# Routed experts' weights in two transfers per expert (8 KB and 4 KB a partition) in place of three of 4 KB

## The reference, cut to what matters

```python
E, K, H, I, CAP = 32, 6, 512, 256, 192
...
xb = jnp.zeros((E, CAP + 1, Hd), x.dtype).at[eid, pos].set(h_rep)
g = jnp.einsum('ech,eih->eci', xb, w_gate)
u = jnp.einsum('ech,eih->eci', xb, w_up)
inter = jax.nn.silu(g) * u
yb = jnp.einsum('eci,ehi->ech', inter, w_down)
y = yb[eid, pos] * w_slot[:, None]
routed = y.reshape(-1, K, Hd).sum(axis=1)
...
x = x + 0.5 * ffn(layernorm(x)); x = x + attention(layernorm(x)); x = x + 0.5 * ffn(layernorm(x))
```

## Time and profile before

| | us |
|---|---|
| median of 3 runs | 1623.55 (1618.26 to 1630.44) |
| the profiled execution's own time | 1628.87 |
| its span, first to last instruction | 1626.6 |
| TensorE busy | 1474.5 (91% of the span) |
| VectorE busy | 1106.5 (68%) |
| ScalarE busy | 1026.9 (63%) |
| GpSimd busy | 777.3 (48%) |
| weight transfers, issue to landing, median of 192 | 6.2 |

### The profile page before, as it was taken

One profiled execution on the slowest core, in us unless ns is written; L12 is line 12 of the kernel. 1 busy time (PEld: TensorE's weight loads), 2 busy tenths in 40 slices (PEclk: granted clock), 3 DMA queues, 4 the chain that ended last, 5 costly groups with the idle time before them and its releaser, 6 DMA issues.

```text
span 1626.6 us, 23865 instructions
## 1 busy us (share of the span) xinstructions
PE 1474.5 (91%) x8434; PEld 1235.5 (76%) x8436; DVE 1106.5 (68%) x2094; ACT 1026.9 (63%) x2046; POOL 777.3 (48%) x655
## 2 busy tenths in 40 slices
PE   5999989999993889999999999986999989999995
PEld 4877778888882678887887888775787769888884
DVE  5659868776682466766666677664658878886873
ACT  6861548877682467666667666663864338887873
POOL 0113245656764666656556656520113234657564
PEclk9999999999997799999999999999999999999998
DMA  7736479999985101111111121103764549999994
GB/s 278 242 121 206 115 269 325 263 275 254 262 219 88 53 27 40 40 51 54 39 41 52 46 91 46 39 27 110 256 203 146 150 158 306 300 292 257 292 235 62
DMA packets 113204, 257.59 MB, mean 158 GB/s; under 512 B 21216, under 2 KB 22176, under 8 KB 112832
## 3 DMA queue, kind: packets, MB, share of 16 engines
q1 hardware_dynamic: 90560, 204.16, 38.1%
q0 software_dynamic: 22528, 51.92, 15.4%
HBM read 187.27 MB, written 68.76 MB: 157 GB/s over the span
## 4 chain that ended last, share of the span: by engine, by line
PE 38%; DMA 12%; POOL 5%; DVE 5%; issue 3%; ACT 3%; DVEq 1%; POOLq 0%; ACTq 0%; SPq 0%
DMA out<-e_y,slots 11%; PE a_bank L90 4%; PE a_bank L92 4%; PE a_bank L91 4%; POOL out L931 4%; PE a_bank L1615 3%; PE a_wide L1606 2%; PE a_wide L1603 2%; PE a_wide L1607 2%; PE a_bank_o L90 2%; PE a_bank_o L92 2%; PE a_bank_o L91 2%; DVEq L1430 1%; PE d_ps_gate L90 1%; PE a_bank L1582 1%
## 5 line engine op out<-in xcount | busy, mean ns | idle before, releaser
L1022 DVE TENSOR_TENSOR e_w_lo<-e_raw,e_w_hi 128x1024 fp32r<-128x1024 f32 x192 | 234.3, 1221 | 30.2 <-ACT e_w_hi L957 30.2
L1539 POOL TENSOR_SCALAR t_prob<-t_prob,t_inv 128x128 f32<-128x128 f32 (+7 forms) x128 | 111.7, 872 | 222.9 <-DVE t_inv L1437 222.7
L957 ACT ACTIVATE e_w_hi<-e_raw 128x1024 fp32r<-128x1024 f32 x192 | 202.3, 1055 | 0.0
L924 POOL DMA_INDIRECT e_xg<-htab,slots x128 | 148.7, 1162 | 73.6 <-issue 35.1
L1096 PE MATMUL e_ps_gate<-e_xt,e_w_hi 128*128 128x384 f32 x512 | 165.9, 387 | 0.0
L406 POOL TENSOR_SCALAR d_inter<-d_inter 128x512 f32<-128x512 f32 x32 | 26.4, 825 | 262.6 <-DVE d_inter L537 262.4
L931 POOL DMA_INDIRECT x_after_ffn<-e_y,slots x64 | 107.7, 1682 | 91.4 <-DMA x_after_ffn<-e_y,slots 80.5
L1096 PE MATMUL e_ps_up<-e_xt,e_w_hi 128*128 128x384 f32 x512 | 151.2, 360 | 0.0
L931 POOL DMA_INDIRECT out<-e_y,slots x64 | 103.7, 1621 | 85.5 <-DMA out<-e_y,slots 74.8
L1327 ACT ACTIVATE t_prob<-a_wide,t_neg_max,a_q_scale 128x128 f32<-128x128 f32 (+7 forms) x128 | 106.5, 832 | 55.6 <-DVE t_neg_max L1431 55.4
L1097 PE MATMUL e_ps_gate<-e_xt,e_w_lo 128*128 128x192 f32 x512 | 133.1, 260 | 0.0
(11 more groups left out here) (218 smaller groups left out, 4464.0 us busy)
## 6 DMA issues: line engine op xcount, KB each, us to landing
e_raw<-in_w_experts SPq DMA_DIRECT2D x192, 512.0 KB, 6.2
htab<-d_h SPq DMA_DIRECT2D x16, 1024.0 KB, 5.2
d_x<-in_x SPq DMA_DIRECT2D x16, 512.0 KB, 6.9
d_xs<-in_x SPq DMA_DIRECT2D x32, 256.0 KB, 3.6
x_after_ffn<-d_xs SPq DMA_DIRECT2D x32, 256.0 KB, 3.3
q_x<-x_after_ffn SPq DMA_DIRECT2D x32, 256.0 KB, 3.0
t_res<-x_after_ffn SPq DMA_DIRECT2D x32, 256.0 KB, 2.7
x_after_attention<-t_res SPq DMA_DIRECT2D x32, 256.0 KB, 2.0
```

Source lines behind the costliest of these rows:

```text
L924: pool.indirect_dma_start(xg[e % GATHERED][q][:, :], None, htab, row).then_inc(gathered[e % GATHERED], 16)
L957: act.activation(third(w_hi[e % 2], c), third(raw[e % 3], c), ACT.Copy).then_inc(hi_ready, 1)
L1022: dve.tensor_tensor(third(w_lo[e % 2], c), third(raw[e % 3], c), third(w_hi[e % 2], c).bitcast(F32), ALU.subtract).then_inc(lo_ready, 1)
L1539: pool.tensor_scalar(prob[:, u, 0:width(i)], prob[:, u, 0:width(i)], inv[:, u:u + 1], 1.0, ALU.mult, ALU.mult).then_inc(p_ready, 1)
```

## The change

The thirds are no longer one transfer each. `LOADS` has two pieces: columns 0 to 2047 (gate and up, 8 KB a partition, 1 MB) and 2048 to 3071 (down, 4 KB a partition, 512 KB). SP issues two transfers an expert. The first one of expert e+3 waits until thirds 0 and 1 of expert e are split (`lo_ready` at 3e+2), the second until third 2 is (3e+3). The splits stay three; those of thirds 0 and 1 both wait for the first transfer. There are 2 semaphores in place of 3 for each buffer.

```diff
--- before.py
+++ after.py
@@ -65,6 +65,7 @@
 NO_SLOT = 4000.0
 SBUF_END = 229344
 THIRD = WALL // 3
+LOADS = (slice(0, WGU), slice(WGU, WALL))
 WORK_AT = SBUF_END - 2 * 4 * WALL - 4 * 8 * NT * E
 GATHERED = 5
 WQKV = KB * 6 * DH
@@ -383,8 +384,7 @@
             spot()
             for u in range(2):
                 sp.wait_ge(up_ready, FB * (PLACES - 2 + u) + FB)
-                for c in range(3):
-                    part = slice(c * THIRD, (c + 1) * THIRD)
+                for c, part in enumerate(LOADS):
                     sp.dma_start(raw[u][:, part], a["w_experts"][u, :, part]).then_inc(w_loaded[u][c], 16)
                 spot()
             sp.wait_ge(w_done, 1)
@@ -896,21 +896,21 @@
         @block.sync
         def _(sp):
             def load_weights(e, c):
-                sp.dma_start(third(raw[e % 3], c), third(a["w_experts"][e, :, :], c)).then_inc(w_loaded[e % 3][c], 16)
+                sp.dma_start(raw[e % 3][:, LOADS[c]], a["w_experts"][e, :, LOADS[c]]).then_inc(w_loaded[e % 3][c], 16)
 
             def load_chunk(c):
                 sp.dma_start(xs[c % XS][:, :], attention_chunks[c][2]).then_inc(att_loaded[c % XS], 16)
 
             sp.wait_ge(done.dense, FB * G)
             sp.wait_ge(gathered[1], 32)
-            for c in range(3):
+            for c in range(2):
                 load_weights(2, c)
             for c in range(min(XS, len(attention_chunks))):
                 sp.wait_ge(y_stored[c], 16 * ((NT - 1 - c) // XS + 1))
                 load_chunk(c)
             for e in range(E - 3):
-                for c in range(3):
-                    sp.wait_ge(lo_ready, 3 * e + c + 1)
+                for c in range(2):
+                    sp.wait_ge(lo_ready, 3 * e + c + 2)
                     load_weights(e + 3, c)
                 if XS <= e + XS - 2 < len(attention_chunks):
                     sp.wait_ge(att_split, e - 1)
@@ -953,7 +953,7 @@
         @block.scalar
         def _(act):
             def split(e, c):
-                act.wait_ge(w_loaded[e % 3][c], 16 * (e // 3) + 16)
+                act.wait_ge(w_loaded[e % 3][c // 2], 16 * (e // 3) + 16)
                 act.activation(third(w_hi[e % 2], c), third(raw[e % 3], c), ACT.Copy).then_inc(hi_ready, 1)
 
             def turn(e):
@@ -1677,7 +1677,7 @@
                 staged = [staged_buffers(nc, places, "place", PLACES - 2 + u, n) for u in range(2)]
                 raw = [nc.alloc_sbuf_tensor_at(f"e_raw{u}_{n}", [P, WALL], F32, offset=staged[u][0]) for u in range(2)]
                 xs = [places.enter_context(nc.sbuf_tensor(f"d_xs{u}_{n}", [P, D], F32)) for u in range(XS)]
-                w_loaded = [[own_semaphore(nc, k, f"e_w_loaded{r}{c}_{n}") for c in range(3)] for r in range(3)]
+                w_loaded = [[own_semaphore(nc, k, f"e_w_loaded{r}{c}_{n}") for c in range(2)] for r in range(3)]
                 y_stored = [own_semaphore(nc, k, f"d_y_stored{u}_{n}") for u in range(XS)]
                 done = front(nc, block, a, k, n, normed, acc, (x1, out), htab, slots, staged, raw, xs, w_loaded, y_stored)
                 routed_experts(nc, block, a, k, n, htab, acc, slots, raw, xs, w_loaded, y_stored, done)
```

## The result

The changed kernel takes 1649.06 us (median of 4 runs, 1640.26 to 1657.33) against 1622.68 for the kernel before (4 runs). The ratio is 1.0144, 95% interval 1.0107 to 1.0181: slower, by some 23 us by the ratio and 26.4 us by the medians. The profiled execution has a span of 1644.7 us against 1626.6, so it shows 18.1 us of the loss.

The account below looks back on a forecast made before the run. The prediction took the ring of scatter landings to bound the expert loops. It summed (0.36 - 0.08) x 49 loops = +13.7 us on the median of 1623.55, giving 1637 us, with a range from 1603 to 1664.

Parts of the forecast that it names:

- What bounds the kernel: Expert loops: a ring of waiting for landings and issuing two scatters, 9.01 us each in FFN 0, 8.72 in FFN 1.
- Items 1 to 3: SP's weight loads and ScalarE's splits: fewer issues, a later first half, and splits awaiting 1 MB; each worth 0.
- leaves later: First half of gate and up is issued 1.60 us later; worth 0, tightest margin 2.1 us in FFN 0.
- Item 4: Weight transfers: larger packets have less overhead, -0.08 us a loop, 3.9 us at most over 49 loops.
- Item 5: Scatters beside weights: longer packets hold them up; +0.36 us a loop taken, between 0 and 0.66, upper end 0.88.
- A: Expert loops: scatters held up a little more, +13.7 us, 1637 us; own range 1626 to 1656; chance 0.40.
- The mechanism inside item 5: Shared engines: a scatter is held up by some 8.5 weight packets, half of an expert's packets becoming 155 ns longer.
- The sign that would have put the gathers into the ring: TensorE waiting much more for gathers while scatters land no later would refute placing gathers outside the ring.
- B: Expert loops: only the packet-overhead saving counts, scatters do not notice packet size; -3.9 us, 1620 us; chance 0.22.
- C: Expert loops: the second scatter finds a gap in the respaced loads; -21 us, 1602 us; chance 0.21.
- D: Queue q0, both expert loops: the scatter loses every engine turn, landings above 6.9 us; +39 us, 1663 us; chance 0.14.
- E: Splits wait for late weights as the 2.1 us margin fails; some 5 to 10 us, once; chance 0.03.

Follow-up runs that it names:

- the repeat: The changed kernel itself, run once more beside the kernel before; 1650.10 us, ratio 1.0194.
- three_2k: Kernel before with the weights laid out in HBM as six blocks of 2 KB rows, same three transfers; 1621.03 us, ratio 0.9993.
- one_4k_later: Changed kernel with one 1.5 MB transfer an expert in 4 KB packets, issued when third 1 of the next expert is split; 1633.68 us, ratio 1.0039.
- late3: Kernel before, but the transfer of third 0 waits until third 1 is split, as in the changed kernel; 1629.60 us, ratio 1.0039.
- even_odd_8k: Kernel before with gate and up loaded as even and odd partitions in 8 KB rows, both when third 1 is split; 1624.07 us, ratio 0.9986.
- two_4k: Changed kernel with weights in 4 KB blocks in HBM, so the 1 MB transfer has 4 KB packets; 1631.65 us, ratio 1.0068.
- one_12k: Changed kernel with one 1.5 MB transfer an expert in 12 KB rows, issued when third 2 is split; 1630.45 us, ratio 1.0040.
- one_2k: Changed kernel with one 1.5 MB transfer an expert in 2 KB packets (six blocks in HBM); 1647.00 us, ratio 1.0127.
- one_4k: Changed kernel with one 1.5 MB transfer an expert in 4 KB packets, issued when third 2 is split; 1614.88 us, ratio 0.9941.
- halves_8k: Kernel before with gate and up loaded as partitions 0 to 63 and 64 to 127 in 8 KB rows, when third 1 is split; 1734.83 us, ratio 1.0683.

## Why the prediction was right, and where it was not

*What bounds the kernel*: right. The changed kernel's loss has the size of the growth of the wait for landings, in both profiled executions (19.0 us of waits for 18.1 of span, 14.0 for 13.6 in the repeat), the halves' loss is mostly there too, and without weights the loops fall to TensorE's 7.99. In small steps the two do not always go together: `three_2k` waits 16.5 us less than the kernel before with a span 6.4 shorter, `one_4k_later` waits the same with a span 4.5 longer.

*Items 1 to 3, worth nothing*: right for waits on loads (0.0 us before line 957, the 2.1 us of margin held). But "leaves later" was priced as lateness alone. `late3` shows 5 to 6 us from the new moment by itself, barely clear of nothing, and `even_odd_8k` with the same timing shows none. That is the likely missing part of the sum: a load that nobody waits for can still collide.

*Item 4, -0.08 a loop*: nothing in the runs shows it as a gain; it is below what they can tell.

*Item 5, the term that carried the forecast*: the sign was right and `two_4k` shows that the long packets of this transfer are its larger part. The size was off. It was put at +0.36 a loop, with item 4 at 0.28 or 13.7 us. Measured were 18.7 us in the 49 loops of one execution, 0.45 a loop in FFN 0 and 0.31 in FFN 1, and in the repeat 0.12 and 0.51, so the share of either FFN is not to be trusted. The loss is some 23 to 26 us by the first measurement, 24 to 31 by the repeat: 12 to 20 of it go with the packets, 7 to 11 with the moment and the one large transfer. 12 to 20 us over 49 loops are 0.25 to 0.41, so the packets' term was about met. That is luck: 0.36 was chosen between 0 and 0.66, and the count of packets behind it is not what the runs show. One slip in the recorded sums: the upper end of A's range, +32, is 0.66 x 49 without the 0.08 of item 4; with it the end is +28. The first measurement lies under both.

*The mechanism inside item 5* was too simple. It had each scatter held up by so many packets of such a length. The median landing stayed at 6.3 us in one execution (6.4 to 6.8 were expected) and was 6.6 in the repeat. What grew in both is the mean landing of the second scatter, with more long ones among them, and about a third of that is a single engine that finishes late while others idle. `even_odd_8k` shows that length alone is not enough, `one_12k` that the loss does not grow with the length as was expected (15.6 us for 35 to 60), and `one_2k` that shorter is not always better. What about the 1 MB transfer of 128 rows of 8 KB makes scatters land late is open; so is whether it is the order in which an engine gets the rows, or the partitions that they go to.

*The other signs*: the loops of FFN 1 took 9.03 us (8.9 to 9.1 expected), ScalarE never waited for weights, and 128 transfers are listed. Queue q1's share fell from 57.0 to 52.8%, more than the point expected, and q0's did not rise (43.7 to 43.3%): the engines idled instead. The sign that would have put the gathers into the ring half appeared, since TensorE waited for them 45.1 us in place of 29.7, but scatters did land later in the mean and GpSimd waited no longer for `e_y`.

*The rivals.* B had the queue indifferent to the packets' size: `two_4k` against the changed kernel speaks against it. C's idea, that the moment of the load matters, holds: `one_4k` against `one_4k_later` is worth 16 to 19 us. But it had the wrong sign for this change, whose new moment costs by `late3`, and that a scatter finds a gap is not shown. D needed landings above 6.9 us; the median did not get there (6.3 and 6.6), the mean of the second scatters just did (7.00 and 6.90), and the 1663 us did not come. E did not happen.

## What to carry to other kernels

When a chain of small dependent transfers sets the pace, a bulk load that nobody waits for is not free: its moment, its rows and its partitions each moved this kernel by 5 to 110 us, while ScalarE's wait for weights stayed under 2 us in all of them but `halves_8k` (12.2). Read the mean landing of the transfer that the chain waits for, over all loops: the median over both scatters, and the longest, misled here. Repeat the profile before a small shift is read from it. Of the loads tried, one transfer an expert in 4 KB rows, issued with the split of third 2, is the best: 1614.88 us, 0.6% under the kernel before (0.9908 to 0.9973).

## What the runs showed of the hardware that was not expected

- Two transfers of 64 partitions, lower and upper half, cost 7% (1734.83 us), and as even and odd partitions nothing (1624.07), with packets of equal number and size. The Trainium skill, "DMA: Bandwidth & Descriptors", Rules for kernel authors, advises against transfers to disjoint partition halves, as they use the same engines anyway. The run agrees with the advice; the even and odd pair shows that it is the halves, not the splitting, that costs: the halves' 8 KB packets take a median of 586 ns, those of the pair 324.
- The rule of the Trainium skill, "DMA: Bandwidth & Descriptors", Rules for kernel authors, to have at least 1 MiB in a transfer for the highest bandwidth does not decide here: with 512 KB transfers the kernel took 1621 to 1630 us (1735 in halves), with 1 MB 1649 and 1632, with 1.5 MB 1615, 1630, 1634 and 1647.
- A single engine can finish some 3 us behind the others: in the pair of scatters shown, 31 of 32 semaphore updates had come by 1406.65 us and the last at 1409.88, with 0.94 of an engine busy on q0 and some thirteen idle.
